# Experts: the down product in plain fp32 in place of three fp32r products

## The reference

```
x = x + 0.5 * ffn(layernorm(x)); x = x + attn(layernorm(x)); x = x + 0.5 * ffn(layernorm(x))
# ffn:
gu = jnp.einsum('th,ehf->tef', x, gate_up_proj) + gate_up_proj_bias     # 256 -> 512
act = (up + 1.0) * glu                       # glu = gate * sigmoid(1.702 gate), clipped
down = jnp.einsum('tei,eih->teh', act, down_proj) + down_proj_bias      # 256 -> 256
out = jnp.einsum('te,teh->th', w, down)
```

## Time and profile before

| what | value |
|---|---|
| timed runs, median (3 runs) | 704.48 us |
| timed runs, lowest and highest | 702.71 and 705.45 us |
| profiled execution, span from first to last instruction | 799.3 us |
| mean granted TensorE clock in it | 0.913 of full |
| TensorE matmuls busy | 631.0 us, 79% |
| TensorE weight loads busy | 527.1 us, 66% |
| VectorE, GpSimd, ScalarE busy | 446.0, 353.5, 314.2 us |
| down product, three lines, 284 rows each | 96.7, 83.2, 83.4 us |

### The profile page before, as it was taken

How to read it: one execution, slowest core, us unless ns; L and a number is a source line. 1 busy time by engine, 2 the same in 40 slices (tenths; PEclk the granted TensorE clock), 3 DMA queues, 4 the chain that set the end, 5 groups by cost and what they waited for, 6 DMA issues and landing times.

```text
span 799.3 us, 13210 instructions
## 1 busy us (share of the span) xinstructions
PE 631.0 (79%) x3712; PEld 527.1 (66%) x3713; DVE 446.0 (56%) x1116; ACT 314.2 (39%) x696; POOL 353.5 (44%) x379
## 2 busy tenths in 40 slices
PE   2673898888878879969998996679898898888900
PEld 2452777776757668858887994568777786767700
DVE  6868653444434436277775986845353444445446
ACT  2663243434333335346663443334243334333400
POOL 2781646565656553513331000155656565656400
PEclk9985999999999998999999999599988999999955
DMA  9871232222222221245542431132212222222179
GB/s 307 295 229 28 73 99 81 70 78 69 85 72 78 78 73 52 93 135 157 157 142 94 150 116 66 8 87 67 79 62 85 70 82 69 79 72 79 54 261 369
DMA packets 52601, 87.99 MB, mean 110 GB/s; under 512 B 16228, under 2 KB 32019, under 8 KB 52054
## 3 DMA queue, kind: packets, MB, share of 16 engines
q1 hardware_dynamic: 17568, 39.52, 15.0%
q0 software_dynamic: 13664, 35.42, 14.3%
q10 hardware_dynamic: 21334, 12.61, 5.1%
HBM read 53.94 MB, written 35.39 MB: 112 GB/s over the span
## 4 chain that ended last, share of the span: by engine, by line
PE 61%; DVE 13%; another core or an unknown queue 8%; DMA 7%; issue 5%; ACT 4%; POOL 0%; SPq 0%; ACTq 0%; DVEq 0%; POOLq 0%
PE ps L854 15%; PE ps L852 13%; PE ps L853 12%; PE ps L843 9%; PE ps L1070 3%; DMA work<-y_dram 3%; PE ps L847 3%; DVE aT_lo L1447 2%; PE ps L877 2%; ACT aT_hi L689 2%; DVE xs L1503 1%; DMA raw_c<-L_ffn_down_proj 1%; PE ps L926 1%; PE ps L869 1%
## 5 line engine op out<-in xcount | busy, mean ns | idle before, releaser
L521 POOL DMA_INDIRECT y_dram<-work,sidx x142 | 142.7, 1005 | 166.7 <-ACT work L706 128.7
L513 POOL DMA_INDIRECT work<-xn_dram,gidx x142 | 140.2, 988 | 47.2 <-issue 43.6
L1455 DVE TENSOR_SCALAR work<-ps 128x256 f32<-128x256 f32 x142 | 57.1, 418 | 147.3 <-issue 83.3
L843 PE MATMUL ps<-cst,work 128*128 128x128 f32 x688 | 109.4, 284 | 29.9 <-DVE aT_lo L1447 22.5
L852 PE MATMUL ps<-up_hi,xT_hi 128*128 x284 | 120.9, 426 | 13.5 <-issue 11.2
L854 PE MATMUL ps<-up_hi,xT_lo 128*128 x284 | 114.1, 402 | 8.6 <-issue 8.2
L853 PE MATMUL ps<-up_lo,xT_hi 128*128 x284 | 113.8, 401 | 8.5 <-issue 7.8
L696 ACT ACTIVATE work<-ps 128x256 f32<-128x256 f32 x142 | 52.1, 393 | 171.7 <-PE ps L854 129.8
L843 PEld LDWEIGHTS ps<-cst,work 128*128 128x128 f32 x688 | 84.3, 145 | 52.3 <-issue 35.3
L852 PE MATMUL ps<-dn_hi,aT_hi 128*128 x284 | 96.7, 340 | 0.0
L706 ACT ACTIVATE work<-ps,slot_gate 128x256 f32<-128x256 f32 x142 | 59.5, 471 | 72.2 <-PE ps L854 54.7
(11 more groups left out here) (172 smaller groups left out, 1136.5 us busy)
## 6 DMA issues: line engine op xcount, KB each, us to landing
work<-y_dram SPq DMA_DIRECT2D x32, 512.0 KB, 4.3
xn_dram<-work ACTq DMA_DIRECT2D x29, 255.0 KB, 2.6
xs<-L_attn_x SPq DMA_DIRECT2D x4, 1024.0 KB, 10.5
work<-q_dram SPq DMA_DIRECT2D x16, 256.0 KB, 2.8
out<-xs SPq DMA_DIRECT2D x16, 256.0 KB, 5.9
q_dram<-work ACTq DMA_DIRECT2D x15, 256.0 KB, 2.3
work<-xn_dram,gidx POOLq DMA_INDIRECT x142
y_dram<-work,sidx POOLq DMA_INDIRECT x142
```

The costliest lines, as they stand in the source:

```text
L513: pool.indirect_dma_start(xg[:, k, u, 1:H + 1], None, xn_dram[n], bass.IndirectOffsetOnAxis(ap=gidx[:, 2 * s + u:2 * s + u + 1], axis=0)). ...
L521: pool.indirect_dma_start(y_dram[n], bass.IndirectOffsetOnAxis(ap=sidx[:, 2 * s + u:2 * s + u + 1], axis=0), ysb[:, k, u, :], None, bounds ...
L843: ins = nc.tensor.transpose(ps[:, bank, k:k + P], src[:, u, c * P:(c + 1) * P], ident)
L1455: return v.tensor_scalar(upv[:, u, :], ps[:, 2 + 2 * b + u, :].rearrange("p (f c) -> p f c", c=2)[:, :, 1], 1.0 - LIMIT, 1.0 + LIMIT, ALU. ...
```

## The change

The down product is made by one plain fp32 matmul a chunk, on the down weights as they come from memory and on the transposed activations as ScalarE copies them out. There are no high and low parts of either. SyncE loads the down weights straight to their place (`dn_w`), on a semaphore of their own that TensorE waits for before the experts; the raw buffers hold the up weights alone and are free when their low part is made. ScalarE's `a_hi` becomes `a_out`, into one fp32 tile `aT`; VectorE's `a_lo` is gone, and TensorE waits for `a_out` instead (`a_sb`). VectorE's first clip of a step waits for the transposes of the activations two steps back (`a_T`), since `a_lo`, which stood behind them, no longer does.

```
--- before.py
+++ after.py
-                sp.dma_start(raws[RAW_OF[e]][:, KC * F:KC * (F + H)].rearrange("p (c f) -> p c f", c=KC),
-                             Wdn[e].rearrange("(c p) f -> p c f", p=P)).then_inc(loaded, 16)
+                sp.dma_start(dn_w[:, :, e, :], Wdn[e].rearrange("(c p) f -> p c f", p=P)).then_inc(dn_loaded, 16)
...
-                low(up_w[1][:, :, e, :], raws[RAW_OF[e]][:, 0:KC * F].rearrange("p (c f) -> p c f", c=KC), up_w[0][:, :, e, :])
-                pool.wait_ge(raw_hi, e + 1)
-                low(dn_w[1][:, :, e, :], raws[RAW_OF[e]][:, KC * F:KC * (F + H)].rearrange("p (c f) -> p c f", c=KC),
-                    dn_w[0][:, :, e, :]).then_inc(raw_lo, 1)
+                low(up_w[1][:, :, e, :], raws[RAW_OF[e]].rearrange("p (c f) -> p c f", c=KC),
+                    up_w[0][:, :, e, :]).then_inc(raw_lo, 1)
...
-                high_down(e)
...
-                if n == 0:
-                    act.wait_ge(raw_loaded[RAW_OF[LAST]], 96 * RAW_OF.count(RAW_OF[LAST]))
-                    high_down(LAST)
...
-                def a_hi(s, b):
+                def a_out(s, b):
                     act.wait_ge(l.a_T, s + 1)
                     wait(act, l.y_ps, s - 1)
                     n = halves(s)
-                    nc.scalar.activation(aTb[b][0][:, 0:n],
-                                         ps[:, 6, :].rearrange("p (u c t) -> p u c t", u=2, c=KC)[:, 0:n], ACT.Copy).then_inc(l.a_hi, 1)
+                    nc.scalar.activation(aT[:, b, 0:n],
+                                         ps[:, 6, :].rearrange("p (u c t) -> p u c t", u=2, c=KC)[:, 0:n], ACT.Copy).then_inc(l.a_sb, 1)
...
                 pe.wait_ge(raw_lo, LAST)
-                pe.wait_ge(raw_hi, LAST)
+                pe.wait_ge(dn_loaded, 16 * E)
...
                     pe.wait_ge(l.act, s + 1)
-                    wait(pe, l.a_lo, s)
+                    wait(pe, l.a_sb, s)
                     transpose4(6, act_v[:, b], halves(s)).then_inc(l.a_T, 1)
...
-                    pe.wait_ge(l.a_lo, s + 1)
+                    pe.wait_ge(l.a_sb, s + 1)
...
-                            ins = product(o, aTb[b][0][:, u, c, :], aTb[b][1][:, u, c, :],
-                                          dn_w[0][:, c, bass.ds(e[u], 1), :], dn_w[1][:, c, bass.ds(e[u], 1), :],
-                                          c == KC - 1)
+                            ins = nc.tensor.matmul(o, aT[:, b, u, c, :],
+                                                   dn_w[:, c, bass.ds(e[u], 1), :].rearrange("p a f -> p (a f)"),
+                                                   start=False, stop=c == KC - 1)
...
-                dve.wait_ge(raw_loaded[RAW_OF[e]], 96 * RAW_OF[:e + 1].count(RAW_OF[e]))
+                dve.wait_ge(raw_loaded[RAW_OF[e]], 80 * RAW_OF[:e + 1].count(RAW_OF[e]))
...
-                v.tensor_tensor(dn_w[1][:, :, LAST, :], last_down, dn_w[0][:, :, LAST, :].bitcast(F32),
-                                ALU.subtract).then_inc(last_lo, 1)
...
                     if u == 0:
                         wait(dve, l.act, s)
+                        wait(dve, l.a_T, s - 1)
...
                     activate(s, b)
-                    a_lo(s - 1, 1 - b)
```

More of the change, by code:

```diff
@@ L176, in build @@
         up_w = [sb(f"up_{h}", [P, KC, E, F], F32R) for h in ("hi", "lo")]
-        dn_w = [sb(f"dn_{h}", [P, KC, E, H], F32R) for h in ("hi", "lo")]
+        dn_w = sb("dn_w", [P, KC, E, H], F32)
         qk_w = [sb(f"qk_{h}", [P, KC, 2 * H], F32R) for h in ("hi", "lo")]
@@ L183, in build @@
         up_bias = sb("up_bias", [E, F], F32)
-        raw_c = sb("raw_c", [P, 1536], F32)
+        raw_c = sb("raw_c", [P, 1024], F32)
         rows_c = sb("rows_c", [P, 2, H], F32)
         xT = [sb(f"xT_{h}", [P, 2, 2, KC, P], F32R) for h in ("hi", "lo")]
-        aT = [sb(f"aT_{h}", [P, 2, KC, P], F32R) for h in ("hi", "lo")]
-        aT2 = [sb(f"aT2_{h}", [P, 2, KC, P], F32R) for h in ("hi", "lo")]
+        aT = sb("aT", [P, 2, 2, KC, P], F32)
         cst = sb("cst", [P, NCONST], F32)
@@ L234, in build @@
         first_rows = [first_row[:, b, :] for b in range(2)] + [area(6208, F)]
-        raws = [area(3136, 1536), area(4672, 1536), raw_c[:, :]]
+        raws = [area(3136, 1024), area(4672, 1024), raw_c[:, :]]
         xn_f = [area(at, 2, H) for at in (0, 512, 6720, 7232)] + [rows_c[:, :, :]]
@@ L245, in build @@
         ysb = area(4616, RING, 2, H)
-        aTb = [[t[:, :, :, :] for t in pair] for pair in (aT, aT2)]
         ybuf = area(0, 4, 2, TOPK, H)
@@ L283, in build @@
         logits_made, logit_T_made, logits_turned_made = sem("logits_made"), sem("logit_T_made"), sem("logits_turned_made")
-        raw_hi = sem("raw_hi")
+        dn_loaded = sem("dn_loaded")
         raw_lo = sem("raw_lo")
@@ L325, in __init__ @@
                 self.gu, self.glu, self.act = s("gu"), s("glu"), s("act")
-                self.a_T, self.a_hi, self.a_lo = s("a_T"), s("a_hi"), s("a_lo")
+                self.a_T, self.a_sb = s("a_T"), s("a_sb")
                 self.y_ps, self.y_sb = s("y_ps"), s("y_sb")
@@ L717, in step @@
                         half_glu(s, b, 1)
-                    a_hi(s - 1, 1 - b)
+                    a_out(s - 1, 1 - b)
                     if not (isinstance(s, int) and s < 2):
@@ L741, in experts @@
                 half_glu(NP - 2, 0, 0)
-                a_hi(NP - 3, 1)
+                a_out(NP - 3, 1)
                 y_last(NP - 4)
@@ L745, in experts @@
                 y_last(NP - 3)
-                a_hi(NP - 2, 0)
+                a_out(NP - 2, 0)
                 half_glu(NP - 1, 1, 0)
                 y_last(NP - 2)
-                a_hi(NP - 1, 1)
+                a_out(NP - 1, 1)
                 y_last(NP - 1)
@@ L1184, in fold @@
             def fold(e):
-                dve.wait_ge(raw_loaded[RAW_OF[e]], 96 * RAW_OF[:e + 1].count(RAW_OF[e]))
-                fold_rows(raws[RAW_OF[e]][:, 0:KC * F].rearrange("p (c f) -> p c f", c=KC),
+                dve.wait_ge(raw_loaded[RAW_OF[e]], 80 * RAW_OF[:e + 1].count(RAW_OF[e]))
+                fold_rows(raws[RAW_OF[e]].rearrange("p (c f) -> p c f", c=KC),
                           first_rows[ROW_OF[e]]).then_inc(folded, 1)
-            last_up, last_down = [raws[RAW_OF[LAST]][:, a:b].rearrange("p (c f) -> p c f", c=KC)
-                                  for a, b in ((0, KC * F), (KC * F, KC * (F + H)))]
+            last_up = raws[RAW_OF[LAST]].rearrange("p (c f) -> p c f", c=KC)
             last_row = first_rows[ROW_OF[LAST]]
@@ L1196, in last_low @@
                 dve.wait_ge(up_hi, KC * E)
-                dve.wait_ge(raw_hi, E)
                 for c in range(KC):
-                    v.tensor_tensor(up_w[1][:, c, LAST, :], last_up[:, c, :], up_w[0][:, c, LAST, :].bitcast(F32),
-                                    ALU.subtract)
-                v.tensor_tensor(dn_w[1][:, :, LAST, :], last_down, dn_w[0][:, :, LAST, :].bitcast(F32),
-                                ALU.subtract).then_inc(last_lo, 1)
+                    ins = v.tensor_tensor(up_w[1][:, c, LAST, :], last_up[:, c, :], up_w[0][:, c, LAST, :].bitcast(F32),
+                                          ALU.subtract)
+                ins.then_inc(last_lo, 1)
             def fold_rows(w, row):
@@ L1442, in x_lo @@
                                     xT[0][:, b, 0:n].bitcast(F32), ALU.subtract).then_inc(l.x_lo, 1)
-                def a_lo(s, b):
-                    dve.wait_ge(l.a_hi, s + 1)
-                    n = halves(s)
-                    v.tensor_tensor(aTb[b][1][:, 0:n],
-                                    ps[:, 6, :].rearrange("p (u c t) -> p u c t", u=2, c=KC)[:, 0:n],
-                                    aTb[b][0][:, 0:n].bitcast(F32), ALU.subtract).then_inc(l.a_lo, 1)
                 def clip(s, b, u):
@@ L1492, in experts @@
                 x_lo(NP - 1, 1, (NP - 1) % RING)
[L1493 to L1494 removed]
+                activate(NP - 2, 0)
                 activate(NP - 1, 1)
[L1496 removed]
             def combine(l, g, j, k, between=None):
```

11 lines of the change are left out of this document (2 added, 9 removed).

## The result

| | before | after |
|---|---|---|
| time, us (median; lowest to highest) | 704.14 (702.71 to 705.45, 4 runs) | 718.85 (718.28 to 719.45, 4 runs) |
| ratio | | 1.0205, 95% interval 1.0185 to 1.0226 |
| profiled execution, us (span) | 799.3 span | 718.28 (716.5) |
| first up product of the experts, us | 90.24 | 84.45 |
| first up to last down product, layer one, two | 240.8, 236.1 | 200.5, 200.1 |

The kernel is 14.7 us slower, and the forecast was 20 us slower, 724. The profiled execution of after is one of the timed ones. The trace of before is 95 us longer than the timed runs beside it, so the two traces can't be subtracted from each other; a step can be compared only with a clean step.

The account below looks back on a forecast made before the run. TensorE was taken to bound the kernel, in clean expert steps. Terms of +23.6 (down product), -1.6 (pipeline drain), -0.6 and -1.0 (start) gave +20.4 us on 704.48, so 724.9, taken as 724; 8-in-10 range 703 to 731.

Parts of the forecast that it names:

- The step: Experts: TensorE sets a clean step; two fp32 products replace six fp32r rows, +0.166 us a tile.
- 23.6 - 1.6: Experts: +23.6 us for the down product over 142 tiles, less 0.8 us a layer where the pipeline drains.
- The start: Before the experts: no down-weight parts and earlier loads; -0.6 for VectorE's row, -1 for all the rest.
- the 0.6: VectorE's down-weight row at 89.08, right before the first tile's low part that the first up product awaits: -0.6 us.
- worth nothing by itself: GpSimd losing fourteen down-weight rows at the start: no gain, as it was done at 63.4 us, then idle 19.16.
- 20.4: Whole kernel: the predicted sum of changes, 23.6 - 1.6 - 0.6 - 1.0 = +20.4 us, giving 724.9.
- The assumption on the stops: Experts: TensorE's stops in every second step belong to the profiled execution; a timed step is a clean one, 5.28 us.
- second rival: Experts: the chain through `aT_lo` sets the timed step, so the kernel gets faster, 691 us (680 to 700); chance 0.10.
- 142 x 0.166: Experts: sign of being wrong if timed time moves by less than this, the down product's extra time over all tiles.
- GpSimd as the holder of the step: Experts: GpSimd's transfers, 5.1 us a step, hide TensorE's extra work: partly, 708 to 716, 0.14; wholly, 701 to 708, 0.11.
- Dearer fp32 rows: Experts' down product: fp32 rows cost more than at L1070, +4 to +8, 728 to 732 us; above 731, chance 0.02.
- Weight loads as TensorE's pace: Experts: an fp32 row costs only its load, 0.117, so -0.23 us a tile and 668 us; chance 0.03.

Follow-up runs that it names:

- e8: Kernel before with all GpSimd indirect gathers and scatters replaced by as many plain SyncE copies: 699.47 us, against 811.13 for the kernel before.
- e9: Changed kernel with all GpSimd indirect gathers and scatters replaced by as many plain SyncE copies: 712.02 us, against 811.13 for the kernel before.
- e6: Changed kernel with the down weights' load counted with the up weights' load again, as before: 788.92 us, ratio 0.9885 to the kernel before.
- e7: Changed kernel with down load counted with up load, plus unused down-weight parts made again on ScalarE and GpSimd: 789.92 us, ratio 0.9873 to the kernel before.
- e4: Kernel before with down weights loaded in place, three fp32r products kept, their parts made after the up weights': 809.86 us, ratio 1.0028 to the kernel before.
- e11: Kernel before with down weights loaded in place, fp32r products kept, GpSimd's low parts delayed until the one-hot rows start: 814.99 us, ratio 1.0052 to the kernel before.
- e12: Kernel before with only the 142 gathers as plain SyncE copies, scatters still indirect: 703.10 us against 703.43, ratio 0.9981, on a third chip.
- e1: Kernel before, unchanged, run again to look for stops in timed executions: 811.25 us, ratio 1.0039 to the kernel before beside it.
- e5: Changed kernel, unchanged, run again on the second chip: 783.62 us against 798.93, ratio 0.9824 to the kernel before.
- e3: Kernel before without VectorE's low part of the activations, third product taking the high part again: 801.79 us, ratio 0.9940 to the kernel before.
- e2: Kernel before with only the down product made plain fp32, on the high parts: 797.24 us, ratio 0.9879 to the kernel before.
- e10: Kernel before, unchanged, one profiled run beside the two kernels with plain copies: 811.7 us.

## Why the prediction came out as it did

**The step: right.** It took the price of an fp32 row from two other lines of the kernel, 0.217, and said 0.985 us a half and a step of 5.60 for 5.27. Measured: 0.98 and 5.58. By e8 and e9 the experts of a layer are 10.0 and 9.9 us longer (189.7 to 199.7, 189.8 to 199.7), so 19.9 in all; the prediction's 23.6 - 1.6 is 22.0. The rest is in two pieces: a tile costs (5.58 - 5.27) / 2 = 0.156, not 0.166 (-1.4 over 142 tiles), and the ends of the layers give a little more than the 0.8 us each that was set for them (71 x 0.156 = 11.1 against 10.0).

**The start: the mechanism right, the size wrong.** "The later loads start earlier ... and mostly move the queue. I take -1 for all of it beyond the -0.6, bounds 0 and -4" is the step that failed. The first up product came 5.8 us earlier by the two traces, 5.6 by e8 and e9, so some 5 beyond the 0.6, outside those bounds. By e6 most of it is folds that needn't wait for down weights, some 5 us. The parts' work on ScalarE and GpSimd may be the rest: e7 puts it at 3.4 us, no more than the scatter between traces, so its size stays open. The row of 2.51 us at 48.49 was read as what the queue would take back. It was on the path, as e6 shows: folds, up weights' copies and the last layer-norm rows take turns on VectorE and ScalarE, and the routing starts behind all of them. And GpSimd's work was "worth nothing by itself" because it ended 19 us before its result was needed; e4 and e11 show that it isn't free for VectorE, which runs beside it.

**The sum.** Between e8 and e9, spans of 696.6 and 709.2: +19.9 in the experts, -5.6 at the start, -0.8 between the layers, -0.9 after them, together 12.6. That is 7.8 under 20.4: -4.0 is the start, -2.1 the experts and -1.7 the two pieces that were not in the sum at all. The real kernels give 14.7, as the indirect transfers cost the changed kernel 6.8 us over its version with plain copies and the one before 4.7, taken across chips or occasions. There is no trace of before without stops, so where these 2.1 us lie is not settled. The nearest is e12, whose scatters are indirect: from it to after the parts are +21.1 in the experts, -4.3 at the start, -1.9 between the layers and +0.1 after them, together 15.1. So the sum missed by 5.7 us: 7.8 one way in terms that it had or left out, and 2.1 back, which was not in it either and brought it closer by luck.

**The assumption on the stops: right for the runs at hand, wrong in its reason, and lucky.** "That the stops belong to the profiled execution" held for the timed runs of the first comparison: 704 is a kernel without stops. But e1 to e11 show three occasions, over 60 runs of the kernel before, in which each run takes 792 us or more, and there the changed kernel is 1.8% faster (e5). The comparison happened to fall where there were none, and that decided the sign. The prediction named that as what would prove it wrong ("then the stops were in the timed runs too"), with 0.10 for its second rival. That rival's mechanism is only a part of it: taking `aT_lo` away gave 0.6% (e3), and the fp32 product, which makes TensorE's work longer, gave 1.2% (e2), so the wait on `aT_lo` passed on a delay that begins elsewhere. Shown: where there are stops, they go when SyncE's plain copies take the place of GpSimd's indirect transfers (e8, e9). Not shown: whether it is the indirect form, the engine that issues them or the rows that they move, whether gathers or scatters do it, what decides on a chip or an occasion, and how they delay what reaches ScalarE.

**A sign of being wrong that was set wrongly.** The prediction calls itself wrong "if timed time moves by less than the 142 x 0.166 that the rows give". That is 23.6 us, more than its own sum of 20.4, and the measured 14.7 is under it too, although the rows cost what it said: the sign left out the gains that the sum had.

**The other rivals.** GpSimd as the holder of the step is out: after has steps of exactly the TensorE sum, and e12 halves GpSimd's work for nothing. Dearer fp32 rows: no, 0.217. Weight loads as TensorE's pace: no. The changed kernel has 284 loads fewer, and without stops its load time falls by 2 us (510.9 in e8, 508.9 in e9), but its step is longer by what the matmul rows cost. The 668 was worked out by taking the measure of the Trainium skill ("Perfetto Trace Analysis", Identifying the Most-Contended Engine) for the bound: the page judges TensorE's headroom by the loads' busy share, with the useful arithmetic, and not by matmul busy time. The trace disagrees with that use of it: in layer one's experts of after the loads are busy for 165.4 of 200.6 us, and TensorE, with matmuls in 199.1 of them, had nothing left.

## What to carry to other kernels

Price a change of matmul kind by the start-to-start distance of rows of that kind and shape that the kernel already has; it was exact to 0.02 us a step. Where a profiled execution is much longer than the timed ones, don't take the difference for an effect of profiling: here its stops were real in other sets of runs, and the same edit is 2.1% slower without them and 1.8% faster with them, so compare the two kernels on an occasion of each sort. A wait for a load in the middle of a chain of small rows on two engines moves all that follows, even when the bytes are the same.

## What was not expected of the hardware

- One kernel on one chip: 811 us with 284 indirect transfers on GpSimd's queue, 699 us with as many plain ones on SyncE's. On another chip the kernel with the indirect ones takes 703.4, about 4 us over that 699 in a comparison across chips.
- Where the stops are, the trace lacks the landings of all indirect transfers and names "remote" as the releaser of ScalarE, 101.8 us in 28 waits in e10:

```profile
ACT work L696 <- remote: 101.8, 28, 4.7
```

- Beside GpSimd's element-wise subtractions most short VectorE rows take about 0.4 to 0.53 us more (0.29 to 0.69, 0.45 to 0.98, 0.68 to 1.21), but not all: 128x256 from fp32 to bf16 keeps its 0.42 (60.11 in e4). The Trainium skill ("GPSIMD Engine Reference", Specifications) says that GpSimd's interfaces to SBUF are shared with VectorE, with contention for VectorE instructions that have two SBUF inputs or run in a two-port mode. The three lengthened rows named here have two SBUF inputs, and so has the row that keeps its 0.42, so the rule alone doesn't say which rows pay. Rows of one input, 128x64, went from 0.20 to 0.56 and 0.65 (68.70 and 69.30 in e4); no trace tells their mode.
